# Flamingo block on one core: opening copies in another order, LoRA factors split kind by kind, one copy for three parts of a fold operand

## The reference

```python
x = x + tanh(g_xattn[0]) * xattn(layernorm(x), ctx, ctx, Wq, Wk, Wv)
x = x + tanh(g_ffn[0])   * ffn(layernorm(x), Wg, W1, b1, A1, B1, W2, b2, A2, B2, W3, b3, A3, B3)

# xattn: q, k, v are three projections; q and k are rotated and scaled by tables; no softmax
out = ((q @ k.T) * decay_mask) @ v
# ffn: 8 experts, the best two of a softmax over x @ Wg.T, with normalised gates
h1 = x @ W1[e].T + (x @ A1[e].T) @ B1[e].T + b1[e]      # A, B: LoRA factors of rank 16
h3 = x @ W3[e].T + (x @ A3[e].T) @ B3[e].T + b3[e]
y_e = (silu(h1) * h3) @ W2[e].T + (.. @ A2[e].T) @ B2[e].T + b2[e]
y = sum over the two experts of gate_e * y_e
```

## Time and profile before

| | us |
|---|---|
| median of three runs | 335.25 |
| the three runs | 332.76, 335.25, 338.57 |
| the profiled execution | 333.05 |
| its span (first to last instruction) | 331.0 |
| attention steps 0 to 7, routing | about 0 to 128 |
| the 39 tiles | about 126 to 319 |

### The profile page before, as it was taken

One profiled execution on the slowest core, in us unless ns is written; L12 is line 12 of the kernel. 1 busy time (PEld: TensorE's weight loads), 2 busy tenths in 40 slices (PEclk: granted clock), 3 DMA queues, 4 the chain that ended last, 5 costly groups with the idle time before them and its releaser, 6 DMA issues.

```text
span 331.0 us, 7183 instructions
## 1 busy us (share of the span) xinstructions
PE 299.9 (91%) x1755; PEld 232.2 (70%) x1755; DVE 199.6 (60%) x533; ACT 202.8 (61%) x486; POOL 206.6 (62%) x253
## 2 busy tenths in 40 slices
PE   7478999978999688999999999999999999999970
PEld 3367777867888554876777777777777777777750
DVE  3488778878899985555665754445445444544530
ACT  5616556646688746869575566557656655765640
POOL 4356868868888138887576566556656755665341
PEclk9699997999999959999999999999999999999996
DMA  7943979869996219124432333332333224244100
GB/s 262 365 134 88 296 221 293 272 199 311 327 286 205 66 35 325 56 35 66 66 56 45 65 61 47 56 60 33 53 62 56 38 50 67 44 51 61 18 0 0
DMA packets 28265, 39.98 MB, mean 121 GB/s; under 512 B 6960, under 2 KB 16564, under 8 KB 27956
## 3 DMA queue, kind: packets, MB, share of 16 engines
q1 hardware_dynamic: 12436, 21.62, 21.2%
q0 software_dynamic: 7488, 9.36, 17.6%
q10 hardware_dynamic: 8304, 8.56, 8.2%
HBM read 27.35 MB, written 10.78 MB: 115 GB/s over the span
## 4 chain that ended last, share of the span: by engine, by line
PE 49%; DMA 2%; ACT 1%; issue 1%; POOLq 1%; ACTq 0%; DVE 0%; POOL 0%
PE bank L615 28%; PE bank L632 14%; PE bank L623 4%; PE bank L605 2%; DMA out<-ys,cols 2%; POOLq L90 1%; ACT L944 0%; ACT h L924 0%; ACT gh L866 0%; DVE ys L1519 0%; ACTq L898 0%; ACT ys L907 0%; POOLq L1021 0%; ACT gsel L884 0%; PE bank L685 0%
## 5 line engine op out<-in xcount | busy, mean ns | idle before, releaser
L1070 POOL DMA_INDIRECT out<-ys,cols x39 | 62.6, 1604 | 62.0 <-DVE ys L1519 47.4
L1508 DVE TENSOR_TENSOR gl<-bank,gh 128x512 fp32r<-128x512 f32 x39 | 27.0, 692 | 63.2 <-ACT gh L866 63.2
L866 ACT ACTIVATE gh<-bank 128x512 fp32r<-128x512 f32 x39 | 23.3, 598 | 65.0 <-PE bank L623 65.0
L615 PE MATMUL bank<-WH,xh 128*128 x156 | 55.3, 435 | 0.0
L971 POOL TENSOR_TENSOR WL<-stage,WH 128x512 bf16<-128x512 f32 x38 | 47.9, 1277 | 10.3 <-ACT WH L732 10.1
L1047 POOL DMA_INDIRECT xg<-xn_rows,colg x39 | 39.3, 1009 | 20.4 <-POOL colg L1025 10.3
L615 PE MATMUL bank<-WH,xl 128*128 x156 | 48.9, 395 | 0.0
L615 PE MATMUL bank<-WL,xb 128*128 x156 | 47.2, 384 | 0.0
L1513 DVE TENSOR_TENSOR g<-bank,h 128x512 f32<-128x512 f32 x39 | 27.0, 691 | 27.7 <-ACT h L924 27.7
L732 ACT ACTIVATE WH<-stage 128x512 fp32r<-128x512 f32 x38 | 23.0, 629 | 22.1 <-DVE stage L1105 19.5
L615 PEld LDWEIGHTS bank<-WH,xl 128*128 128x128 f32 x156 | 29.2, 188 | 6.3 <-DVE xl L1504 0.4
(11 more groups left out here) (232 smaller groups left out, 647.0 us busy)
## 6 DMA issues: line engine op xcount, KB each, us to landing
stage<-w_all_in SPq DMA_DIRECT2D x38, 256.0 KB, 5.3
WL<-w_all_in SPq DMA_DIRECT2D x10, 256.0 KB, 4.9
LS<-WH SPq DMA_DIRECT2D x45, 48.0 KB
xn_rows<-xn ACTq DMA_DIRECT2D x8, 255.0 KB, 5.0
out<-x ACTq DMA_DIRECT2D x7, 256.0 KB, 4.1
cx<-ctxT_in ACTq DMA_DIRECT2D x6, 256.0 KB, 5.8
lora_parts<-WH ACTq DMA_DIRECT2D x3, 432.0 KB, 6.2
LS<-lora_parts SPq DMA_DIRECT2D x9, 144.0 KB
```

Of the source, the lines that this page charges most:

```text
L615: last = nc.tensor.matmul(dst[:, :], lhs[p][:, c * P:(c + 1) * P], W[:, bass.ds(e * (UNITS * UC) + (2 * kind + c) * UC, HID)], start=(part ...
L866: nc.scalar.activation(gh[:], pG[:, :], ACT.Copy).then_inc(s_gh, 1)
L1070: nc.gpsimd.indirect_dma_start(out=out_rows, out_offset=bass.IndirectOffsetOnAxis(ap=cols[:, i:i + 1], axis=0), in_=ys[p][:], in_offset=No ...
L1508: nc.vector.tensor_tensor(gl[:], pG[:, :], gh[:].bitcast(F32), ALU.subtract).then_inc(s_gl, 1)
```

## The change

In SP's opening the copy of q's weights moves from behind the factors to the sixth place, ahead of v's weights; each of them has a semaphore of its own (`s_qw`, `s_vw`), as have q's tables (`s_qtab`) and the mask with the router's weights (`s_msk`). The factors come in three copies, one for each kind, with q's tables between the first and the second, and the small copies for the bias rows between the second and the third.

The work on the factors is split by kind. In step 0, DVE lifts kinds 0 and 1 and makes the rests of kind 0 ahead of the rotation of q; the rests of kind 1 and the bias rows come behind it, and those of kind 2 in step 1, ahead of the mask product. ACT rounds and pairs kinds 0 and 1 where it did all three, and kind 2 behind the copy of v. POOL rotates k first, then makes the rest of kind 1, rotates q, then makes that of kind 2. SP's first operand of a kind waits for that kind only, and ACT's three stores to DRAM wait for all kinds.

For experts 0 to 4, one copy fills the 48 rows of an operand from the three parts, seen as one array of 16 partitions by 3 by 768. The rows then stand in another order, which the product does not notice.

```diff
-                for part in range(3):
...
+                if s == 0:
+                    sp.wait_ge(s_lround, 2 * (kind + 1))
+                    sp.wait_ge(s_lrestA, kind + 1)
+                    sp.wait_ge(s_lrestB[kind], 1)
+                sp.dma_start(LS[lb][0:LROWS, :].bitcast(F32), lparts[s * R:(s + 1) * R, :, cols].bitcast(F32)).then_inc(s_ls[lb], 16)
...
+        lparts = WH[:, KEPT * KINDS * WCOL:E * KINDS * WCOL].rearrange("p (a w) -> p a w", a=3)[:, :, 0:KINDS * LCOL]
...
-            sp.dma_start(ident[:], ident_in).then_inc(s_vtab, 16)
-            sp.dma_start(wq[:, 2], wqkv[:, 2]).then_inc(s_vtab, 16)
-            sp.dma_start(lraw, lora).then_inc(s_lraw, 16)
+            sp.dma_start(ident[:], ident_in).then_inc(s_id, 16)
+            sp.dma_start(wq[:, 0], wqkv[:, 0]).then_inc(s_qw, 16)
+            sp.dma_start(wq[:, 2], wqkv[:, 2]).then_inc(s_vw, 16)
+
+            def load_raw(kind):
+                cols = slice(kind * LCOL, (kind + 1) * LCOL)
+                sp.dma_start(lraw[:, cols], lora[:, cols]).then_inc(s_lraw[kind], 16)
+
+            load_raw(0)
+            sp.dma_start(tab_q[:], tables[:, 0:2]).then_inc(s_qtab, 16)
+            load_raw(1)
             for kind in range(2):
                 rows = slice(2 * kind * E, 2 * (kind + 1) * E)
                 sp.dma_start(last_raw[rows][0::2], w_all[:, 2 * kind + 1, P - 1, :]).then_inc(s_last_in, 16)
                 sp.dma_start(last_raw[rows][1::2], biases[:, kind * HID:(kind + 1) * HID]).then_inc(s_last_in, 16)
-            sp.dma_start(wq[:, 0], wqkv[:, 0]).then_inc(s_tab, 16)
-            sp.dma_start(tab_q[:], tables[:, 0:2]).then_inc(s_tab, 16)
-            sp.dma_start(msk, mask).then_inc(s_tab, 16)
-            sp.dma_start(wg[:], wgT).then_inc(s_tab, 16)
+            load_raw(2)
+            sp.dma_start(msk, mask).then_inc(s_msk, 16)
+            sp.dma_start(wg[:], wgT).then_inc(s_msk, 16)
 
             load_x(1)
             load_ctx(1, 1)
...
                 if not two:
-                    pe.wait_ge(s_tab, 4 * 16)
+                    pe.wait_ge(s_qw, 16)
                 pe.wait_ge(s_xnT, s + 1)
...
+                if not two:
+                    pe.wait_ge(s_vw, 16)
                 pos_wait(pe, s_v, s)
...
+            def round_factors(kind):
+
+                act.wait_ge(s_ldiff, kind + 1) if kind < 2 else act.wait_ge(s_lraw[kind], 16)
+                cols = slice(kind * LCOL, (kind + 1) * LCOL)
+                nc.scalar.activation(lpart[0][:, cols], lraw[:, cols], ACT.Copy).then_inc(s_lhi, 1)
+                for part, (a, b) in ((1, lB[kind]), (2, lA[kind])):
+                    nc.scalar.activation(lpart[part][:, a:b], lraw[:, a:b], ACT.Copy).then_inc(s_lround, 1)
...
                 if s == 0:
-                    round_factors()
-                    pair_factors()
+                    round_factors(0)
+                    round_factors(1)
...
                 nc.scalar.activation(v[u][:].rearrange("p t d -> p (t d)"), pV[:, :], ACT.Copy).then_inc(s_v, 1)
+                if s == 0:
+                    round_factors(2)
...
-            pool.wait_ge(s_lhi, 1)
-            for a, b in lB[1:]:
+
+            def factor_rest(kind):
+
+                pool.wait_ge(s_lhi, kind + 1)
+                a, b = lB[kind]
                 nc.gpsimd.tensor_tensor(lpart[2][:, a:b], lraw[:, a:b], lpart[0][:, a:b].bitcast(F32), ALU.subtract
-                                        ).then_inc(s_lrest[1], 1)
+                                        ).then_inc(s_lrestB[kind], 1)
...
                 rotated(kT, s_kT)
+                if s == 0:
+                    factor_rest(1)
...
                 rotated(qT, s_qT)
+                if s == 0:
+                    factor_rest(2)
...
                 if s == 0:
-                    lifted_factors()
-                    factor_rests()
-                    rows_of_last()
+                    lifted_factors(0)
+                    lifted_factors(1)
+                    factor_rests(0)
                 else:
...
+                if s == 1:
+                    factor_rests(2)
+                    dve.wait_ge(s_msk, 2 * 16)
                 if two:
                     masked(s)
...
                 if s == 0:
-                    dve.wait_ge(s_tab, 4 * 16)
+                    dve.wait_ge(s_qtab, 16)
                 dve.wait_ge(s_qproj, s + 1)
                 dve.wait_ge(s_kT, 2 * (s + 1))
                 rotate(pQ, 0, 0)
                 rotate(pQ, 0, 1, s_qrot)
+                if s == 0:
+                    factor_rests(1)
+                    rows_of_last()
```

More of the change, by code:

```diff
@@ L291, in ls_loads @@
             if s == E - 1 and kind == KINDS - 1:
-                return E * 4 * 16 + 16 + 3 * 16
-            return (s + 1) * 4 * 16 + 16 if kind < 2 else (s + 1) * 3 * 16
+                return E * 2 * 16 + 16 + 16
+            return (s + 1) * 2 * 16 + 16 if kind < 2 else (s + 1) * 16
         def settle(eng):
@@ L378, in load_factors @@
                 if s >= KEPT:
-                    sp.dma_start(LS[lb][0:LROWS, :].bitcast(F32), lora_d[s - KEPT, :, cols]).then_inc(s_ls[lb], 3 * 16)
+                    sp.dma_start(LS[lb][0:LROWS, :].bitcast(F32), lora_d[s - KEPT, :, cols]).then_inc(s_ls[lb], 16)
                     return
-                for part in range(3):
[L382 to L389, removed]
+                if s == 0:
[3 more added lines that the diff above has]
+                sp.dma_start(LS[lb][0:LROWS, :].bitcast(F32), lparts[s * R:(s + 1) * R, :, cols].bitcast(F32)).then_inc(s_ls[lb], 16)
             def load_weights(s, u, kind):
@@ L492, in logits @@
             def logits(b, dst):
+                if b == 0:
+                    pe.wait_ge(s_msk, 2 * 16)
                 pe.wait_ge(s_xn2T, b + 1)
@@ L536, in step @@
                 else:
-                    pe.wait_ge(s_vtab, 2 * 16)
+                    pe.wait_ge(s_id, 16)
                 if three:
@@ L705, in store_factors @@
             def store_factors(part):
-                act.wait_ge(s_lhi, 1)
-                if part > 0:
-                    act.wait_ge(s_lround, part)
-                    act.wait_ge(s_lrest[part - 1], KINDS)
+                act.wait_ge(s_lround, 2 * KINDS)
+                if part == 1:
+                    act.wait_ge(s_lrestA, KINDS)
+                if part == 2:
+                    for kind in range(KINDS):
+                        act.wait_ge(s_lrestB[kind], 1)
                 act.dma_start(lora_rows[:, part, :], lpart[part][KEPT * R:E * R, :].bitcast(F32)).then_inc(s_lstore, 16)
@@ L716, in store_last_rows @@
                 act.dma_start(last_d, last_rows.bitcast(F32)).then_inc(s_lstore, 16)
-            def round_factors():
-                act.wait_ge(s_ldiff, 4)
-                nc.scalar.activation(lpart[0], lraw, ACT.Copy).then_inc(s_lhi, 1)
-            def pair_factors():
-                for part, cols in ((1, lB), (2, lA)):
-                    for a, b in cols:
-                        last = nc.scalar.activation(lpart[part][:, a:b], lraw[:, a:b], ACT.Copy)
-                    last.then_inc(s_lround, 1)
+            def round_factors(kind):
[4 more added lines that the diff above has]
+                    nc.scalar.activation(lpart[part][:, a:b], lraw[:, a:b], ACT.Copy).then_inc(s_lround, 1)
             def weight_hi(s, u, m):
```

36 lines of the change are left out of this document (20 added, 16 removed).

## The result

| | before | after |
|---|---|---|
| median of 20 runs, us | 333.25 | 329.95 |
| profiled execution, us | 333.05 | 328.52 |
| its span, us | 331.0 | 326.7 |

The ratio after to before is 0.989, with a 95% interval of 0.986 to 0.992: faster by 1.1%. I had forecast 324.6 us, from gains of 5.1 and 4.4 us; what came is 3.3 us in the medians and 4.3 in the spans of the two profiled executions. The 329.95 us lie inside my range of 320 to 331, but at its far end, where I had put the rivals and not the case that I held likeliest.

What follows compares the result with a forecast made beforehand. PE was taken to bound the tile phase, which the change could only let begin earlier. Off the 333.05 us execution came 5.1 (opening) and 4.4 (steady steps), giving 323.6; with half of 2.2 on top, 324.6 us, range 320 to 331.

Steps and rivals of the forecast that it cites:

- the case that I held likeliest: Both gains come, in the opening and in the steady steps: chance 0.60, a span of times from 322 to 328 us.
- The opening, up to 17 us: Before step 1's operand: q projection at 9.6, context tile and k projection at 15.1, DVE's rotation of step 1 at 17.4.
- Operand 0: First operand of step 1: reaches PE at about 20 to 21 us, level with the mask product and hidden beside it.
- the 1.6 us from the end of the issue to PE: Delay taken for operand 0 in step 1, from the earlier trace: last issue ends at 22.96, PE gets it at 24.56.
- Operand 0 queues behind the six weights just issued, or PE's short idle spells drop the clock in step 1 as at 12 us: Rival on step 1: opening gives 2.0 us, steady part halved to 2.2; 330 us, chance 0.12.
- its lower bound of 3.5: Opening's gain forecast at 5.1 us; 3.5 if context tile or operand comes a us and a half later.
- 1.1 us on top: Added to the forecast execution: half of the 2.2 us by which the median of three runs lay above the profiled execution.
- The merged copy's issue: SP's one copy for three, experts 0 to 4: issue taken as 0.7 us, freeing 3.2 us of SP in each step.
- The steady gain of 4.4: Steps 2 to 5, from SP time freed by the merged copy: 4.4 us, bounds 0 and 5.6.
- 11.83 us is PE's own pace, and what lies above it, or ahead of the first step, can be won: Attention steps: the shortest, 11.83 us with PE busy for 11.38, taken as PE's limit; the five before took 12.55 to 14.09.
- step 3, half of whose lost clock I had counted as won: Steady steps: half of step 3's 1.69 us of lost clock and the rest of its excess, 1.42 us in all.
- Only the opening counts: Rival on the steady steps: SP's freed time goes into waiting for transfers, steps keep their lengths; 329 us, chance 0.22.

Runs made afterwards that it cites:

- e3: Changed kernel with the four staged weights of kinds 1 and 2 of expert 0 issued behind operands 0 and 1; ratio to the kernel before 0.986.
- e6: Changed kernel with ACT's two loads of batch 2 issued one step later, behind the normed x of step 1; 327.28 us, ratio to the kernel before 0.985.
- e2: Kernel before with only the merged copy in place of three for experts 0 to 4, its opening as it was; 332.25 us, ratio 0.995.
- e7: Changed kernel with the loads of batches 3 to 7 issued by SP in place of ACT; 327.47 us, ratio to the kernel before 0.985.
- e11: Changed kernel with SP loading batches 3 to 7 and three part copies for each operand in place of the merged one; 331.74 us, ratio 0.995.
- e8: Changed kernel, merged copies of operands 0 and 1 issued earlier, batches 2 to 7 loaded by SP, 12 filler matmuls in step 1; 328.69 us, ratio 0.989.

## Why the prediction was wrong

**The opening, up to 17 us: right.** The q projection at 9.74 (9.6 forecast), its eight records in 1.97 us at full clock where the earlier trace rows had 3.78; the context tile at 15.16 (15.1); the rotation of step 1 at 17.19 (17.4). The rests of kind 2 took 0.99 us, not the 0.7 taken, within their bounds.

**Operand 0: mis-sized.** SP was even ahead of the forecast (last issue done at 18.11, not "near 19"). The term that failed is the 1.6 us from the end of the issue to PE, read from the earlier trace rows: it measured 3.95. In the kernel before, the last of the six weights had landed by 18.7, before the operand's issue (the DMA share of its step 1 is 0.37); pulled forward, the operand stands behind them and batch 2. e3 and e6 gave 2.84 and 2.70 with less of the crowd, e2 2.59; so the way of the one large copy, counted from the end of its issue, was taken a us too short even without the full crowd. So it came at 22.06 and not at "20 to 21, level with the mask product and hidden beside it", past the 21 us that I had named as a sign of being wrong.

**What a wait of PE costs: counted once, it cost twice.** Behind 3.59 us of idle time came a drop of the clock, 1.5 us more, for which the sum had nothing. I had named it, as a rival ("Operand 0 queues behind the six weights just issued, or PE's short idle spells drop the clock in step 1 as at 12 us", 0.12, 330 us); it joined the two with *or*, and both came. So the opening stayed below its lower bound of 3.5. That rival's sum, 2.0 of the opening and 2.2 of the steady part, is close to the 1.5 and 2.1 measured. That its 330 us meets the 329.95 to a tenth is luck: it has 1.1 us on top for the median, which didn't come, and the times differ by 3.3 us where the spans differ by 4.3.

**The merged copy's issue: right, and better.** 0.58 us (median of 15), not 0.7; SP's time was freed as worked out, and PE's waits for operands went from 3.3 us to none between 28 and 94.

**The steady gain of 4.4: the step that failed is "11.83 us is PE's own pace, and what lies above it, or ahead of the first step, can be won".** It holds three errors. 11.83 us is not PE's own pace: e7 ran four steps at 11.44 to 11.62. The excess of a step over step 6 is not all SP's, as I had put it; ACT's copy of the router's operand is a limit too. Measured from the start of a step's k projection, that copy ends after 4.08, 4.73, 4.27 and 4.21 us in steps 2 to 5 of the kernel after, after 3.49 in step 6, and after 2.96 in three of the four steps of e7 (3.49 in the other). Step 6 has loads of a batch on ACT as well, the last ones, but they were short there, 0.52 us each, where in step 3 the second took 1.56. Timeline of step 6 after:

```profile
82.63 0.52 ACTq L762 DMA_DIRECT2D xs<-x_in  x1
...
83.18 0.52 ACTq L763 DMA_DIRECT2D cx<-ctxT_in  x1
...
84.80 0.57 ACT L756 ACTIVATE xn2T<-bank 128x512 f32<-128x512 f32 x1
```

In the kernel before, the copy was as late (4.44, 4.78, 4.07 and 4.04 us in steps 2 to 5, 3.70 in step 6), and the merged copy changed nothing there: steps 2, 4 and 5 stop at 12.2 to 12.4. Third, step 3, half of whose lost clock I had counted as won, lost it again (0.04 of 1.42 us), behind the same idle spell at the router's operand as before. A wait that the trace named would have been the better measure: PE's waits for operands in the steady steps, 3.3 us in the kernel before, against the 2.1 that came.

**"Only the opening counts"** (0.22) rested on transfers being the limit of the steps. e7 and e11 speak against it: at the same bytes, the time moved by 1.1% with the number of copies that SP issues, and steps 2 to 5 by 8.3 us. The Trainium skill ("DMA: Bandwidth & Descriptors", Issuing engines are not separate DMA queues) calls the time to initiate a copy usually small beside the copy; by that, e11 would have been level with e7. It was not. One issue of 0.59 us is indeed short beside the 3.45 us from operand 0's first issue to its fold in the earlier trace rows, but nine of them in a step add up on SP. The other half of that section of the Trainium skill, that copies of all engines interleave on the same DMA engines, is what e6 shows (0.67 us). Another page of the Trainium skill ("Perfetto Trace Analysis", What "DMA-bound" means) lists the sequencer of the issuing engine, where its track is solid with DMA slices, as a limit of its own. ACT's track is not solid, 15.0 us of issues between 28 and 94, and e7 shows that they were the limit all the same.

**The median.** I laid 1.1 us on top for a median of three runs that lay above the profiled execution; over 20 runs it is 333.25, level with that execution's 333.05.

## What to carry to other kernels

Before a step's excess over the fastest step is put down to one queue, compare in both when each operand of PE's is ready; here the router's operand, which ACT copies, was also earlier in the fastest step, and even that step was not PE's own pace. An engine that computes and issues copies pays for a long issue with its own instructions, so loads that nobody waits for soon are better off on a queue that computes nothing, as far as that queue has time left (e7 against e11). And an earlier start shortens a kernel only as far as the slowest operand comes earlier too: ask for each one what shares the transfers at its new time.

## What was not expected of the hardware

- The issue of a copy went by the copy, not by its bytes: one of 144 KB from three places took SP 0.58 us (median), one of 48 KB 0.59.
- Copies from SBUF into the operands fill the DMA engines at a low rate: 22 to 23 us after shows a share of 0.97 at 98 GB/s, where the earlier trace rows have 1.07 at 396 with loads from DRAM on their way.
- The issue of one and the same copy on ACT varied: the context load of a batch took 0.46 to 1.56 us in the kernel after (six of them, median 1.03), 2.53 once in e3, and the store of the bias rows 0.68 after and 3.12 in e8. The DMA share was 0.99 to 1.23 while the longer ones stood, but it was 1.02 as well around the 0.52 us of step 6, so that a crowd alone makes an issue long is not shown.
- The clock drop often came when PE was busy again, 0.3 to 2.5 us behind an idle spell, and in e7 inside the spell; spells of 3.5 to 3.9 us ended with it and without it, and two of only 0.7 us (step 3 of either kernel) were followed by one. Which spell does it is left open.
